# A two-layer conditional residual block on one core: the start of the kernel with one index table, read by SyncE alone, and the first loads requested in another order

## The reference

```
x = x + (x @ W[cat] + b[cat])              # layer 0: cat = itok_B_0_63[b], W is 64 x 256 x 256
s0 = relu(x @ swi[0]) @ swo[0]             # layer 1: two shared MLPs, 256 -> 1024 -> 256
s1 = relu(x @ swi[1]) @ swo[1]
eo = relu(x @ wi[type]) @ wo[type]         # and one that type = itok_B_0_2[b] selects (of 5)
w  = softmax(relu(concat(eo[:,0], s0[:,0], s1[:,0]) @ g1) @ g2)   # from the first token
x  = x + eo*w[:,0] + s0*w[:,1] + s1*w[:,2]
```

## Time and profile before

| | |
|---|---|
| median of the timed runs | 268.43 us (3 runs, 268.33 to 268.64) |
| the profiled execution's own time | 268.28 us |
| its span, first to last instruction | 266.4 us |
| PE busy in the span | 262.2 us, 98% |
| ACT, DVE, POOL busy | 150.0, 162.7, 162.1 us |
| granted TensorE clock | full in every slice of the span |

### The profile page before, as it was taken

The page is one execution under the profiler, slowest core; times in us unless marked ns, Lnnn a source line. Parts: engine busy times, 40 slices in busy tenths (PEclk is TensorE's granted clock), DMA queues, the critical chain, the costliest instruction groups (busy, mean ns, idle before and its releaser), DMA issues.

```text
span 266.4 us, 3466 instructions
## 1 busy us (share of the span) xinstructions
PE 262.2 (98%) x1160; PEld 217.4 (82%) x1160; DVE 162.7 (61%) x246; ACT 150.0 (56%) x266; POOL 162.1 (61%) x171
## 2 busy tenths in 40 slices
PE   8999999999999999999999999999999999999995
PEld 7788888888888888888888888888888888888884
DVE  3879968635645435644445565345477577985664
ACT  2696357866666555565655744646645755645320
POOL 0379999999958949838944725725626528535000
PEclk9999999999999999999999999999999999999999
DMA  5844322112012112202022112012022022000404
GB/s 154 235 162 160 119 79 80 28 55 80 16 65 79 38 41 79 79 5 79 0 81 79 20 58 81 9 73 79 2 79 79 0 79 80 1 0 0 157 4 158
DMA packets 7473, 18.31 MB, mean 69 GB/s; under 512 B 1312, under 2 KB 2080, under 8 KB 7456
## 3 DMA queue, kind: packets, MB, share of 16 engines
q1 hardware_dynamic: 6592, 16.65, 18.7%
q10 hardware_dynamic: 864, 1.44, 1.7%
HBM read 16.00 MB, written 2.10 MB: 68 GB/s over the span
## 4 chain that ended last, share of the span: by engine, by line
PE 97%; DMA 1%; SPq 1%; issue 0%; DVE 0%; ACT 0%; DVEq 0%
PE acc L730 49%; PE chain L730 23%; PE right L730 12%; PE left L730 6%; PE acc L739 4%; DMA w_raw<-cat_w 1%; SPq L237 1%; PE left L782 1%; PE corner L730 1%; PE right L782 1%; PE corner L782 1%; PE chain L782 1%; DVE x L721 0%; ACT w_hi L373 0%; SPq L239 0%
## 5 line engine op out<-in xcount | busy, mean ns | idle before, releaser
L281 POOL TENSOR_TENSOR m_lo<-staged,m_hi 128x512 fp32r<-128x512 f32 (+2 forms) x49 | 82.9, 1702 | 76.3 <-ACT m_hi L361 62.8
L730 PE MATMUL acc<-h_hi,m_hi 128*128 128x512 f32 x190 | 73.9, 389 | 0.0
L730 PE MATMUL acc<-h_hi,m_lo 128*128 128x512 f32 x190 | 73.9, 389 | 0.0
L730 PE MATMUL acc<-h_lo,m_hi 128*128 128x512 f32 x190 | 73.9, 389 | 0.0
L385 ACT COPY kept<-chain 128x512 f32<-128x512 f32 x66 | 38.9, 589 | 52.8 <-PE chain L730 52.7
L730 PEld LDWEIGHTS acc<-h_lo,m_hi 128*128 128x128 f32 x190 | 35.7, 188 | 7.5
L730 PEld LDWEIGHTS acc<-h_hi,m_lo 128*128 128x128 f32 x190 | 35.7, 188 | 7.4
L730 PEld LDWEIGHTS acc<-h_hi,m_hi 128*128 128x128 f32 x190 | 35.7, 188 | 7.3
L517 DVE SCALAR_TENSOR_TENSOR h_lo<-left,h_hi 128x512 fp32r<-128x512 f32 x24 | 16.6, 690 | 28.4 <-ACT h_hi L397 28.4
L281 POOL TENSOR_TENSOR staged<-staged 128x128 f32<-128x128 f32 x66 | 30.9, 482 | 1.7
L522 DVE TENSOR_TENSOR left<-left,kept 128x512 f32<-128x512 f32 x22 | 15.3, 694 | 23.7 <-PE left L730 23.7
(11 more groups left out here) (149 smaller groups left out, 439.0 us busy)
## 6 DMA issues: line engine op xcount, KB each, us to landing
staged<-mlp_w SPq DMA_DIRECT2D x22, 512.0 KB, 3.3
x<-x_t ACTq DMA_DIRECT2D x4, 256.0 KB, 3.4
x<-x_t SPq DMA_DIRECT2D x4, 256.0 KB, 6.9
out_t<-x SPq DMA_DIRECT2D x2, 512.0 KB, 4.4
staged<-mlp_w SPq DMA_DIRECT2D x3, 256.0 KB, 3.6
g_sb<-g SPq DMA_DIRECT2D x1, 768.0 KB, 3.8
out_t<-x SPq DMA_DIRECT2D x3, 256.0 KB, 2.3
w_raw<-cat_w SPq DMA_DIRECT2D x4, 128.0 KB, 2.9
```

What stands on the lines that cost most here:

```text
L281: return nc.gpsimd.tensor_tensor(out, a, b, ALU.subtract)
L730: last = nc.tensor.matmul(out[:, columns], half[:, slot, at:at + P], moving[:, columns], start=(start and n == 0), stop=(stop and n == 2), ...
```

## The change

The two index vectors become one table `ids` of four entries, categories first. SP alone reads it: it requests x's chunk (0, 0) first, reads the category index without a bounds check, requests the two weight chunks, reads the MLP index, requests the first `wi` group (before, a request of ACT), and then the bias. Before its first `wo` request it waits until x's chunk (t, d) = (1, 1) is there. ACT reads no index and requests chunk (0, 1) at once. ACT's rounding of the first weight chunk is cut in two halves of 128 columns, with a semaphore `w_first_hi` for the first; its rounding of the first 256 columns of `wi` comes before `part_hi_of(0)`. DVE's early work is reordered: the second x chunk is rounded before the first weight rest, and the rest of x's chunk (1, 0) is made before the updated x of (0, 0). POOL's first subtraction also waits for the rest of x's chunk (1, 1). PE does 9 warm-up matmuls.

```
-WARMUP = 10
+WARMUP = 9
+        w_first_hi = sem("w_first_hi")
@@ sync
             def load_layer0(b):
-                cat = sp.value_load(cat_ids[0:1, b:b + 1], min_val=0, max_val=CATS - 1)
+                cat = sp.value_load(ids[0:1, b:b + 1])
                 for d in range(DC):
                     sp.dma_start(w_raw[:, b, d * D:(d + 1) * D], cat_w[bass.ds(cat, 1), :, d].rearrange("a p n -> p (a n)")
                                  ).then_inc(w_loaded[b][d], 16)
+                if b == 0:
+                    first = sp.value_load(ids[0:1, B:B + 1], min_val=0, max_val=EXPERTS - 1)
+                    load_wi(sp, bass.ds(first, 1), 0)
                 sp.dma_start(bias[:, b, :], cat_b[bass.ds(cat, 1)].rearrange("a p d -> p (a d)")).then_inc(bias_loaded[b], 16)
-
-            load_layer0(0)
+                return first if b == 0 else None
+
+            load_x(sp, 0, 0, 0)
+            first = load_layer0(0)
             for q, (kind, _) in enumerate(PASSES):
-                if kind == 0:
-                    mlp = sp.value_load(mlp_ids[0:1, q:q + 1], min_val=0, max_val=EXPERTS - 1)
+                if q == 0:
+                    bank = bass.ds(first, 1)
+                elif kind == 0:
+                    mlp = sp.value_load(ids[0:1, B + q:B + q + 1], min_val=0, max_val=EXPERTS - 1)
...
                 for j in range(q * GROUPS, (q + 1) * GROUPS):
+                    if j == 0:
+                        sp.wait_ge(x_loaded[0][1][DC - 1], 16)
@@ gpsimd
+            pool.wait_ge(x_split[0][1][DC - 1], 1)
             pool.wait_ge(row1_hi_ready, 1)
@@ scalar
-            load_x(act, 0, 0, 0)
+            load_x(act, 0, 0, 1)
             act.wait_ge(ones_ready, 1)
             nc.scalar.activation(table[:], ones[:, 0:1], ACT.Relu)
-            mlp = act.value_load(mlp_ids[0:1, 0:1], min_val=0, max_val=EXPERTS - 1)
-
-            load_x(act, 0, 0, 1)
             act.wait_ge(x_loaded[0][0][0], 16)
             for d in range(DC):
                 load_x(act, 0, 1, d)
-            w_hi_of(0, 0)
-            load_wi(act, bass.ds(mlp, 1), 0)
+            act.wait_ge(w_loaded[0][0], 16)
+            nc.scalar.copy(w_hi[:, 0, 0:P], w_raw[:, 0, 0:P]).then_inc(w_first_hi, 1)
+            nc.scalar.copy(w_hi[:, 0, P:D], w_raw[:, 0, P:D]).then_inc(w_hi_ready, 1)
             w_hi_of(0, 1)
             for d in range(DC):
                 x_hi_of(0, 1, d)
-            part_hi_of(0)
             act.wait_ge(staged_loaded[0], 16)
             nc.scalar.copy(m_hi[:, 0, A11:A22], staged[:, 0, A11:A22]).then_inc(row1_hi_ready, 1)
+            part_hi_of(0)
             nc.scalar.copy(m_hi[:, 0, A22:RAW_S], staged[:, 0, A22:RAW_S]).then_inc(m_hi_ready, 1)
@@ vector
-            for d in range(DC):
+            def x_first_hi_of(d):
                 dve.wait_ge(x_loaded[0][0][d], 16)
                 nc.vector.tensor_copy(x_part(x_hi, 0, 0, d), x1_part(0, 0, d)).then_inc(x_first_hi, 1)
+            def x_first_lo_of(d):
                 dve.wait_ge(x_first_hi, d + 1)
                 subtract(x_part(x_lo, 0, 0, d), x1_part(0, 0, d), x_part(x_hi, 0, 0, d).bitcast(F32)).then_inc(x_split[0][0][d], 1)
-                w_lo_of(0, d)
+            x_first_hi_of(0)
+            x_first_lo_of(0)
+            x_first_hi_of(1)
+            w_lo_of(0, 0)
+            x_first_lo_of(1)
+            w_lo_of(0, 1)
+            x_lo_of(0, 1, 0)
             dve.wait_ge(bias_loaded[0], 16)
             make_x1(0, 0, 0)
-            for d in range(DC):
-                x_lo_of(0, 1, d)
+            x_lo_of(0, 1, 1)
             make_x1(0, 0, 1)
@@ tensor, layer0_first
                     pe.wait_ge(x_first_hi, i + 1)
-                    pe.wait_ge(w_hi_ready, i + 1)
                     for d in range(DC):
+                        if i == 0 and d == 0:
+                            pe.wait_ge(w_first_hi, 1)
+                        else:
+                            pe.wait_ge(w_hi_ready, i + 1)
                         layer0_product(0, 0, i, d, w_hi, x_hi, i == 0, False)
@@ arrays
-        "mlp_ids": np.asarray(itok_B_0_2)[None],
-        "cat_ids": np.asarray(itok_B_0_63)[None],
+        "ids": np.concatenate([np.asarray(itok_B_0_63), np.asarray(itok_B_0_2)])[None],
```

More of the change, by code:

```diff
@@ L44, with build @@
 NTH = [1, 3, 2, 4]
-def build(nc, x_t, cat_w, cat_b, mlp_w, mlp_ids, cat_ids, g1, g2, out_t):
+def build(nc, x_t, cat_w, cat_b, mlp_w, ids, g1, g2, out_t):
     B, _, _, S = x_t.shape
@@ L50, in build @@
     HALVES = S // TOK
-    CATS = cat_w.shape[0]
     BANKS = mlp_w.shape[0]
```

## The result

The change makes the kernel slower: 270.09 us median (269.20 to 270.59, 22 runs) against 268.61 us of the kernel before on the same chips; ratio 1.0045, 95% interval 1.0033 to 1.0056. The forecast was 268.2 (267.6 to 269.1), no change of note. The 22 runs fall into two groups, 10 from 269.20 to 269.57 and 12 from 270.06 to 270.59. The profiled execution took 270.37 us and is of the upper group. Two of the 22 runs of the kernel before are high as well (270.77 and 271.07); no trace of such a run was kept.

What follows compares the result with a forecast made beforehand. PE was taken to bound the kernel, so only its start and early stalls could win. Start 0.0, stalls -0.15 and bias +0.05 made -0.1 us against the profiled 268.28, stated as 268.2 (267.6 to 269.1).

Steps and rivals of the forecast that it cites:

- Term 3: ACT's first rounding in halves: 128 columns take about 0.30 us, gain 0.11; PE starts at 5.78, start gain 0.0.
- the clock rival: PE after fewer warm-ups: a longer gap might end the full clock; no price given; chance 0.02.
- Term 1: SP's first weight request: x request +0.43, register load +0.03, check removed -0.20, so out at 2.91 us (2.82 to 3.05).
- Term 5: The bias behind SP's second register load and the wi request: just in time or 0.35 us late, loss taken 0.05.
- Term 2: Landing of the first weight chunk: 2.40 us (2.3 to 2.57) after its request, at 5.31.
- Term 4: PE's stalls in its first 24 matmuls: 0.15 of 0.26 us won back (0 to 0.26).
- the deadline: DVE's first update of x: the bias must land by 9.13 us for PE's 22nd real matmul at 10.55.
- P + V: SP's second register load, pointer P plus value V, ahead of wi and bias: taken as 1.42 to 1.6 us.
- the rival at 0.22: Late bias: DVE waits ahead of `make_x1(0, 0, 0)` for a bias landing after 9.13; 268.4 to 269.7 us; chance 0.22.
- The floor of the value load: The skill's register-load floor, about 0.6 us: with it the bias goes out 0.12 later, forecast up 0.1.
- Shared stream: x's two first chunks share one stream: the first up to 1.4 us later, PE's 13th matmul 0.9 late, 269.0; chance 0.04.

Runs made afterwards that it cites:

- after_w9_bias: The changed kernel, its 9 warm-ups kept, with the bias requested ahead of SP's second register load; runs from 268.38 to 270.66 us, the profiled one 269.15.
- before_spx: The kernel before with only x's chunk (0,0) requested by SP ahead of the index instead of by ACT; 4.6 us slower, ratio 1.0164.
- after_w11_bias: The changed kernel with 11 warm-ups and the bias requested ahead of SP's second register load; 268.92 us, ratio 1.0004 against the kernel before.
- after_w11: The changed kernel with 11 warm-up matmuls in place of 9, nothing else; 269.46 us, ratio 1.0029 against the kernel before.
- after_w10_actx: The changed kernel with 10 warm-ups and both of x's first chunks requested by ACT, SP starting with the index load; 268.65 us, ratio 0.9987.

## Why the prediction was wrong

**The step that failed** is the end of Term 3, that the gap ahead of the first matmul "costs nothing by itself; the granted clock was full in each stretch read, the first ones included". The 1.00 was read as 2.4 GHz; the warm-ups' own durations (421 ns, the last one 341) were in the trace and said that the level had only just risen when the real work began. The 0.2275 us per warm-up record, which the prediction set beside the 0.227 of a real matmul, is the lower level's too: in the changed kernel the records start 0.21 apart (4.64, 4.85), and in `after_w9_bias`, where the level rises among them, 0.11 (4.07, 4.18). So the clock rival got 0.02 and no price, where over half of the runs pay 0.87 us by it. That the level was low could be read from those rows; how long it would stay down no row of the trace before shows. The lower group, which this step doesn't explain, lies outside the forecast as well: there Terms 1 and 5 failed.

**Term 1, SP's first request**: forecast 2.91, measured 3.55. The x request (0.39) and the value (0.47) are as forecast; the check gave back 0.31, more than the 0.20 taken; the pointer load took 1.68 and not 0.93. The row taken for it was ACT's, and SP's does not behave like it (`before_spx`). This is the mis-sized term of the start. **Term 2, the landing**: 2.13, better than the forecast 2.40. **Term 3, the halves**: 0.31 for 128 columns, as forecast. The start is 6.14 against 5.78. It is what stays in `after_w11_bias`: PE is 0.37 late at its passes in the profile (17.50 against 17.13), 0.44 by the medians, with an interval that holds no change too.

**Term 4, the stalls**: right. 5.74 us for 24 matmuls once nothing else is late.

**Term 5, the late bias**: the place, the deadline and the way were right, the choice of row was wrong. P + V was taken as 1.42 to 1.6 from ACT's row; it measured 2.38, and 2.60 in `after_w11`. Line 246's own pair, 2.69, at the same place on the same engine, was in the text as the other bound and was the nearer row. With it this rival would have come to 269.1 to 269.7; the lower group is 269.20 to 269.57. So the rival at 0.22 was the likelier case, though that its figure fits is in part luck: about 0.4 of the lower group's 0.8 is the late start, which the rival did not have. The floor of the value load, weighed there, did not matter.

**Shared stream**: partly there. Chunk (0,0) reached DVE at 4.37 and not at 3.87, 0.5 late, with both queues at work. It lies beside the weights' longer wait and cost nothing by itself. The argument against it, a higher rate with two queues, doesn't need the second queue: from 2.5 to 2.9 us the two chunks moved 256 GB/s from two queues in the changed kernel and 312 GB/s from ACT's one queue in `after_w10_actx`, against 179 for one chunk before.

In sum, by medians: 0.4 for the late start, 0.5 for the bias in the runs with full pace, and about 0.9 more where the pace is late, in which the bias is hidden.

## What to carry to other kernels

Take the price of a register load from the same engine and the same place in its queue, and check what stands ahead of it; a request put ahead of an index load delays everything that hangs on the index, and a tiny load moved behind a register load can become the last to land. Read PE's level from the durations of the matmuls themselves, not only from the clock column, and when the first real matmul is delayed or warm-ups are cut, time many runs: the loss shows in some of them only. And where two engines read indices, one table for both is worth a test against two: here it cost 0.85 us.

## What was not expected of the hardware

- SP's pointer load: 0.86 to 1.05 us with no request of its own ahead, 1.62 to 2.15 with one 256 KB request ahead. ACT's: 0.91 to 1.15, but 1.73 and 1.77 where SP loads the same pointer.
- After a break of 1.51 us between warm-ups and real work PE ran at 2.4 GHz in one run, and after one of 0.87 us at 1.2 GHz in another of the same kernel, with the same warm-ups before; it rose at 10.2 us there, and at 13.9 us in `before_spx`, judged by the matmuls' spacing.
- A chunk of 128 KB of weights landed in 2.13 to 3.80 us. The x chunks around it are not the whole of it: in two runs of the changed kernel the requests have the same order, and the second chunk landed in 2.7 us in one and in 3.80 in the other.
